# Copying operand stacks, row maxima and attention sums from SBUF to SBUF in a two-layer attention and FFN kernel

## The reference, cut to what matters

```python
x = x + attn_a(layernorm(x))      # (16, 512, 128) float32; 16 heads of 8; causal; three heads re-weighted by token region
x = x + ffn(layernorm(x))         # silu gate, two 512x512 layers with exact gelu, back to 128
x = x + attn_b(layernorm(x))      # 16 heads of 8; rotary; not causal
x = x + ffn(layernorm(x))
# one attention:
scores = einsum('bhqd,bhkd->bhqk', q, k) / sqrt(8)
out = einsum('bhqk,bhkd->bhqd', softmax(scores), v)       # then the output projection
```

## Time and profile before

| | us |
|---|---|
| median of 3 runs (2568.77 to 2573.33) | 2572.24 |
| the profiled execution | 2562.1 |
| its span | 2560.1 |
| attention "a", first maxima to last projection | 60.33 to 850.69 |
| attention "b", the same | 1308.22 to 2149.32 |

### The profile page before, as it was taken

How to read it: one execution, slowest core, us unless ns; L and a number is a source line. 1 busy time by engine, 2 the same in 40 slices (tenths; PEclk the granted TensorE clock), 3 DMA queues, 4 the chain that set the end, 5 groups by cost and what they waited for, 6 DMA issues and landing times. The chain is left out here.

```text
span 2560.1 us, 39181 instructions
## 1 busy us (share of the span) xinstructions
PE 2178.2 (85%) x14018; PEld 1036.9 (41%) x14018; DVE 1750.2 (68%) x2621; ACT 1463.2 (57%) x2948; POOL 984.6 (38%) x1184
## 2 busy tenths in 40 slices
PE   1889888888888599999658998998899874999998
PEld 0323223223222388788511222222222211888886
DVE  5766666666662467666259998998998852667663
ACT  0366556555556255555306777777777773555654
POOL 2445445445443244544332242232233200544543
PEclk8788878888887799999758999999999997999999
DMA  6343433433430000000033334434334310000000
GB/s 169 82 89 76 102 83 80 103 81 85 100 75 20 15 1 1 1 1 1 25 69 81 75 79 93 83 77 99 81 73 99 83 30 15 9 13 12 10 13 13
DMA packets 114582, 147.17 MB, mean 57 GB/s; under 512 B 27600, under 2 KB 88656, under 8 KB 113232
## 3 DMA queue, kind: packets, MB, share of 16 engines
q1 hardware_dynamic: 114384, 144.60, 26.0%
HBM read 78.47 MB, written 66.06 MB: 56 GB/s over the span
## 5 line engine op out<-in xcount | busy, mean ns | idle before, releaser
L586 DVE TENSOR_REDUCE b_negmax<-ps_max 128x2 f32<-128x1024 f32 x512 | 611.9, 1219 | 93.4 <-PE ps_max L700 90.9
L667 ACT ACTIVATE b_prob<-ps_score 128x512 f32<-128x512 f32 x1024 | 547.8, 598 | 196.0 <-PE ps_score L687 194.6
L586 DVE TENSOR_REDUCE a_negmax<-ps_max 128x2 f32<-128x256 f32 (+3 forms) x512 | 410.7, 821 | 225.6 <-PE ps_max L704 221.6
L667 ACT ACTIVATE a_prob<-ps_score 128x512 f32<-128x512 f32 (+3 forms) x1024 | 386.5, 437 | 302.0 <-PE ps_score L687 300.2
L687 PE MATMUL ps_score<-b_stack_q,stack_k 50*128 50x512 bf16 x1024 | 257.8, 388 | 56.1 <-ACT b_prob L667 46.8
L503 POOL TENSOR_SCALAR_AFFINE_SELECT a_prob<-a_prob 128x512 f32<-128x512 f32 x256 | 163.3, 638 | 363.4 <-ACT a_prob L667 363.4
L721 PE MATMUL ps_out<-b_prob,b_v_aug 128*9 128x512 f32 x2048 | 268.6, 596 | 18.9 <-ACT b_o_raw L640 12.9
L700 PE MATMUL ps_max<-stack_k,b_stack_q 48*128 48x512 bf16 x1024 | 233.9, 397 | 35.8 <-DMA stack_k<-d_stack 19.8
L687 PE MATMUL ps_score<-a_stack_q,stack_k 50*128 50x512 bf16 (+3 forms) x1024 | 204.1, 342 | 69.0 <-DMA a_stack_q<-d_nm 63.2
L980 PE MATMUL ps_score<-fa_h,w_hi 128*128 128x512 f32 x1024 | 251.6, 403 | 3.9 <-DVE fa_h L895 2.8
L980 PE MATMUL ps_score<-fb_h,w_hi 128*128 128x512 f32 x1024 | 247.5, 398 | 3.9 <-DVE fb_h L895 2.8
(11 more groups left out here) (136 smaller groups left out, 2946.9 us busy)
## 6 DMA issues: line engine op xcount, KB each, us to landing
stack_k<-d_stack SPq DMA_DIRECT2D x128, 192.0 KB, 4.2
d_stack<-a_parts SPq DMA_DIRECT2D x64, 192.0 KB, 2.8
a_stack_q<-d_stack SPq DMA_DIRECT2D x64, 192.0 KB, 4.5
d_stack<-b_parts SPq DMA_DIRECT2D x64, 192.0 KB, 2.8
b_stack_q<-d_stack SPq DMA_DIRECT2D x64, 192.0 KB, 4.1
d_stack<-a_parts SPq DMA_DIRECT2D x64, 128.0 KB, 2.8
d_stack<-b_parts SPq DMA_DIRECT2D x64, 128.0 KB, 2.8
d_stack<-a_parts SPq DMA_DIRECT2D x64, 64.0 KB, 2.5
```

The lines of the kernel that those rows point to most:

```text
L586: dve.tensor_reduce(m["negmax"][:, t, :, p], dve_banks("max", k)[:, :, 0:keys], AX.X, ALU.max, negate=True).then_inc(s["max"], 1)
L667: act.activation(m["prob"][u % PROBS][:, g, lo:S], act_bank("score", 4 * u + g)[:, 0:S - lo], ACT.Exp).then_inc(s["prob"], 1)
```

## The change

`d_stack`, `d_nm`, `d_num` and `d_den` in DRAM go away. The parts are copied straight into the stacks with 12 DMAs for q and 12 for k (`stack`), each from 64 partitions of `parts` (1 KB on each) to 8 partitions of a stack (8 KB on each). The rows of maxima, the sums and the numerators are copied straight as well; `o_num` in four DMAs, each from 8 partitions of `o_raw` (8 KB on each) to 32 partitions. The reciprocals still go through `d_rden`, read back in four DMAs instead of eight. There are three buffers of each stack instead of two, so that the copies of batch n wait for scores of batch n-3. SP's order becomes `aug(1)`, `numerators`, stack of q, reciprocals out, stack of k, reciprocals back, `aug(0)`. The first maxima of a batch wait for both whole stacks, no longer for a half. ScalarE waits for `den` and `o_in` before it overwrites `o_raw`. The rows of the output weights are reordered to match `o_num`, and the program reserves less scratch for DMAs.

```diff
@@ -44,6 +44,8 @@
 MASKED = -1.0e30
 SCORE_BANKS = 3
 PROBS = 4
+STACKS = 3
+COPIES = 16 * 2 * TERMS
 
 
 W_AT = {"a": 0, "b": F, "h1": 2 * F, "h2": 2 * F + FT * F, "out": 2 * F + 2 * FT * F}
...
-        m["d_stack"] = dram("d_stack", (2, 2, TERMS, HD, PAIRS, S), BF16)
-        m["d_nm"] = dram("d_nm", (2, 2, 2, HALF, S), BF16)
-        m["d_num"] = dram("d_num", (HD, 4, GROUPS, S), F32)
-        m["d_den"] = dram("d_den", (4, GROUPS, S), F32)
         m["d_rden"] = dram("d_rden", (4, GROUPS, S), F32)
...
@@ -347,69 +345,47 @@
             else:
                 sp.dma_start(m["focus"][:], a["focus"]).then_inc(s["focus"], 16)
 
-            def aug(h, b, c):
+            def aug(h, b):
 
                 sp.wait_ge(s[f"nm_row{h}"], b + 1)
-                sp.dma_start(m["d_nm"][h].rearrange("o c p t -> (o c p) t"), m["nm_rows"][:, h, :])\
-                    .then_inc(s["nm_out"], 16)
-
-                sp.wait_ge(s["nm_out"], count(32, b, 16 * (h + 1)))
                 for o in range(2):
                     at = SIDE * o + KROWS
-                    sp.dma_start(m["stack_q"][c][at:at + AUG, HALF * h:HALF * (h + 1), :],
-                                 m["d_nm"][h, o]).then_inc(s[f"aug{h}"], 16)
-
-            def outputs(b):
+                    sp.dma_start(m["stack_q"][b % STACKS][at:at + AUG, HALF * h:HALF * (h + 1), :],
+                                 m["nm_rows"][2 * HALF * o:2 * HALF * (o + 1), h, :]).then_inc(s[f"aug{h}"], 16)
+
+            def numerators(b):
 
                 sp.wait_ge(s["o_raw"], count(GROUPS, b, GROUPS))
+                wait(sp, s["rden"], b)
+                sp.dma_start(m["den"][:], m["o_raw"][HD::32]).then_inc(s["den"], 16)
+                wait(sp, s["oT"], b)
                 for g in range(4):
-                    sp.dma_start(m["d_num"][:, g], m["o_raw"][32 * g:32 * g + HD]).then_inc(s["o_out"], 16)
-                    sp.dma_start(m["d_den"][g:g + 1], m["o_raw"][32 * g + HD:32 * g + HD + 1])\
-                        .then_inc(s["o_out"], 16)
-                sp.wait_ge(s["o_out"], count(128, b, 128))
-                wait(sp, s["rden"], b)
-                sp.dma_start(m["den"][:], m["d_den"].rearrange("g h (c t) -> (g h c) t", c=P // H))\
-                    .then_inc(s["den"], 16)
-                wait(sp, s["oT"], b)
-                sp.dma_start(m["o_num"][:], m["d_num"].rearrange("d g h t -> (d g h) t")).then_inc(s["o_in"], 16)
+                    sp.dma_start(m["o_num"][32 * g:32 * (g + 1)], m["o_raw"][32 * g:32 * g + HD])\
+                        .then_inc(s["o_in"], 16)
+
+            def store_reciprocals(b):
+
                 sp.wait_ge(s["rden"], b + 1)
                 sp.dma_start(m["d_rden"].rearrange("g h (c t) -> (g h c) t", c=P // H), m["rden"][:])\
                     .then_inc(s["rden_out"], 16)
+
+            def spread_reciprocals(b):
+
                 sp.wait_ge(s["rden_out"], count(16, b, 16))
-                for d in range(HD):
-                    sp.dma_start(m["o_rden"][H * d:H * (d + 1), :], m["d_rden"].rearrange("g h t -> (g h) t"))\
-                        .then_inc(s["r_in"], 16)
-
-            def store(b):
-
-                for i, name in enumerate(("stored_q", "stored_k")):
-                    sp.wait_ge(s["parts"], count(2, b, i + 1))
-
-                    wait(sp, s["half0"], count(64, b))
-                    wait(sp, s["half1"], count(64, b))
+                for g in range(4):
+                    rows = m["d_rden"][g:g + 1].broadcast_to([HD, GROUPS, S])
+                    sp.dma_start(m["o_rden"][32 * g:32 * (g + 1)], rows).then_inc(s["r_in"], 16)
+
+            def stack(b, name, i):
+
+                wait(sp, s["score"], count(4 * UNITS, b - STACKS, 4 * UNITS))
+                sp.wait_ge(s["parts"], count(2, b, i + 1))
+                part_of = (0, 0, 0, 1, 1, 2) if i == 0 else (0, 1, 2, 0, 1, 0)
+                for t, part in enumerate(part_of):
                     for o in range(2):
-                        parts = m["parts"][64 * o:64 * (o + 1), i]
-                        rows = m["d_stack"][i, o].rearrange("t d p n -> (d p) t n")
-                        if i == 0:
-                            for part, lo, hi in ((0, 0, 3), (1, 3, 5), (2, 5, 6)):
-                                sp.dma_start(rows[:, lo:hi],
-                                             parts[:, part:part + 1].broadcast_to([64, hi - lo, S]))\
-                                    .then_inc(s[name], 16)
-                        else:
-                            for lo, hi in ((0, 3), (3, 5), (5, 6)):
-                                sp.dma_start(rows[:, lo:hi], parts[:, 0:hi - lo]).then_inc(s[name], 16)
-                sp.wait_ge(s["stored_q"], count(96, b, 96))
-                sp.wait_ge(s["stored_k"], count(96, b, 96))
-
-            def load(b, c, h):
-
-                wait(sp, s["score"], count(4 * UNITS, b - 2, 2 * UNITS * (h + 1)))
-                pairs = slice(HALF * h, HALF * (h + 1))
-                for o in range(2):
-                    q, k = (m["d_stack"][i, o].rearrange("t d p n -> (t d) p n") for i in range(2))
-                    rows = slice(SIDE * o, SIDE * o + KROWS)
-                    sp.dma_start(m["stack_q"][c][rows, pairs, :], q[:, pairs, :]).then_inc(s[f"half{h}"], 16)
-                    sp.dma_start(m["stack_k"][c][rows, pairs, :], k[:, pairs, :]).then_inc(s[f"half{h}"], 16)
+                        at = SIDE * o + HD * t
+                        sp.dma_start(m[name][b % STACKS][at:at + HD],
+                                     m["parts"][SIDE * o:SIDE * (o + 1), i, part]).then_inc(s[name], 16)
 
             if causal:
 
@@ -417,18 +393,20 @@
                     sp.dma_start(raw(i), a["w_" + name].rearrange("(k p) f -> p k f", p=P))\
                         .then_inc(s["w_raw"], 16)
             for n in range(STEPS):
-                c = n % 2
                 if on(n, 2):
-                    aug(1, n - 2, c)
+                    aug(1, n - 2)
                 if on(n, 3):
-                    outputs(n - 3)
+                    numerators(n - 3)
                 if on(n, 0):
-                    store(n)
-                    load(n, c, 0)
+                    stack(n, "stack_q", 0)
+                if on(n, 3):
+                    store_reciprocals(n - 3)
+                if on(n, 0):
+                    stack(n, "stack_k", 1)
+                if on(n, 3):
+                    spread_reciprocals(n - 3)
                 if on(n, 1):
-                    aug(0, n - 1, 1 - c)
-                if on(n, 0):
-                    load(n, c, 1)
+                    aug(0, n - 1)
 
         @block.gpsimd
         def _(pool):
...
-                wait(pool, s["stored_q" if i == 0 else "stored_k"], count(96, b))
+                wait(pool, s["stack_q" if i == 0 else "stack_k"], count(COPIES, b))
...
-                pool.wait_ge(s["o_in"], count(16, b, 16))
-                pool.wait_ge(s["r_in"], count(16 * HD, b, 16 * HD))
+                pool.wait_ge(s["o_in"], count(64, b, 64))
+                pool.wait_ge(s["r_in"], count(64, b, 64))
...
-                wait(act, s["nm_out"], count(32, b - 1, 16 * (h + 1)))
+                wait(act, s[f"aug{h}"], count(32, b))
...
-                wait(act, s["o_out"], count(128, b))
+                wait(act, s["den"], count(16, b))
+                wait(act, s["o_in"], count(64, b))
...
-                b, c = n - 2, n % 2
+                b, c = n - 2, (n - 2) % STACKS
...
-                    pe.wait_ge(s[f"half{h}"], count(64, b, 64))
...
             def maxes(n, k):
 
-                b, c = n - 1, (n - 1) % 2
+                b, c = n - 1, (n - 1) % STACKS
                 p, t = k // T, k % T
-                if k % (MAXES // 2) == 0:
-                    pe.wait_ge(s[f"half{k // (MAXES // 2)}"], count(64, b, 64))
+                if k == 0:
+                    pe.wait_ge(s["stack_q"], count(COPIES, b, COPIES))
+                    pe.wait_ge(s["stack_k"], count(COPIES, b, COPIES))
                 dve_banks_free(pe, n, "max", k)
                 to, keys = dve_banks("max", k), P * (t + 1) if causal else S
                 for o in range(2):
...
-    return np.array([(4 * G + g) * HD + d for d in range(HD) for g in range(4) for G in range(GROUPS)])
+    return np.array([(4 * G + g) * HD + d for g in range(4) for d in range(HD) for G in range(GROUPS)])
...
-    nc = bacc.Bacc("TRN2", target_bir_lowering=False, num_devices=1)
+    nc = bacc.Bacc("TRN2", target_bir_lowering=False, num_devices=1, dynamic_dma_scratch_size=1024)
```

More of the change, by code:

```diff
@@ L101, in program @@
         m["ps_max"] = ctx.enter_context(nc.psum_tensor("ps_max", [P, 4, 512], F32))
[L103 removed]
+        m["stack_k"] = [sb(f"stack_k{c}", [P, PAIRS, S], BF16) for c in range(STACKS)]
         m["ps_hid"], m["ps_misc"] = m["ps_score"][:, 0:2], m["ps_score"][:, 2]
@@ L158, in _ @@
             dve.memset(m["ps_out"][:], 0.0)
-            for c in range(2):
+            for c in range(STACKS):
```

(2 more changed lines are left out.)

7 lines of the change are left out of this document (3 added, 4 removed).

## The result

The changed kernel takes 2754.47 us (median of 4 runs, 2745.7 to 2758.44), the kernel before 2571.89 (4 runs): a ratio of 1.0707, 95% interval 1.0679 to 1.0735, 182.6 us slower. The profiled execution has a span of 2752.3 us against 2560.1.

The account below looks back on a forecast made before the run. It took the first attention to be bound by the wait for maxima and its half clock, no DMA bounding the second; 108 + 122 + 35 - 10 = +255 us on 2562.1 gave 2817, median 2827 us, range 2570 to 2995.

Parts of the forecast that it names:

- The price of a copy: Each 64 KB copy from 64 partitions to 8 takes 1.02 us, bounds 0.32 to 1.23; 24 take 24.5 us per step.
- the narrow stretch: Stretch from 835.7 to 840.2 in the earlier trace, four 64 KB copies from 8 partitions, 64 GB/s at DMA share 0.45.
- overlap between the halves: Consecutive copies, below and above partition 64 in turn, run beside each other: 0.55 us a copy, 2472 us; both fast cases 0.20.
- The reciprocals: Four DMAs spreading reciprocals, behind the copies in SP's queue: 3.0 us, four issues and 1.8 to land, before POOL's product.
- First attention: Copies, reciprocals, product, mask and two units form a loop: 55.4 us per step against 47.07, +108 us over 13 steps.
- the half clock that it put on the next step's start: First attention: of 3.7 us lost to half clock after unit 14's wait, 2.2 fall on the next step's start.
- Second attention: TensorE's projection in unit 14 waits for the product: 58.3 us per step against 48.88, +122 us over 13 steps.
- First batches: First maxima of the attentions +6.6 and +8.7 us later, the next two steps of each +5 each; together +35 us.
- Last batches: End of both attentions: without the DRAM hop, outputs to product take 10.9 us instead of 15.7; -10 us together.
- At nothing: Parts counted as costing nothing: third stack buffer, SP's 38 DMAs, ScalarE's new wait, larger clearing, first maxima's wait for whole stacks.
- The cheap rivals: Copies are cheap and the kernel faster: 0.32 us a copy gives 2446 us, 0.55 gives 2472; chance 0.20 for both.
- The break-even: Below 0.65 us per copy, about 100 GB/s, faster wins; there the two attention loops together equal 47.07 and 48.88 us.

Follow-up runs that it names:

- the best version: Changed kernel with rows six partitions apart and SP's order four q copies, reciprocals out, eight q copies, reciprocals spread, maxima, k's copies: 2499.47 us, ratio 0.9699.
- a better order: Changed kernel, rows still side by side, with reciprocals sent out within q's copies and reciprocals and maxima ahead of k's copies: 2574.38 us, ratio 0.9991.

## Why the prediction was right, and where it was off

It forecast 2827 us in a range of 2570 to 2995, slower at 0.77. Measured is 2754, in the direction and by the mechanism that it named, 28% less than the +255 us of its sum.

- **The price of a copy**, taken as 1.02 us from the narrow stretch of the earlier trace rows, is 0.92 by the windows of a slow step, about 0.7 in the fastest (91 to 104 GB/s), so the forecast had the slow end of it. Whether overlap between the halves, which it chose to ignore, makes the difference is not shown. With the reciprocals it said 27.5 us from q's part to the product; the trace has 26.0 at 341.61 and, in the second attention, 27.8 (1542.85 + 1.16 + 27.8 = 1571.81), but 24.7 and 26.1 in the mean of each attention's 13 steps.
- **The reciprocals**, taken as 3.0 us, were too cheap: with the copies bound by SP's issue, in the kernel with rows six apart, their way takes some 5.5. Copies too dear and reciprocals too cheap cancel in part in the 27.5; that part of the agreement is luck.
- **First attention**, 55.4 us per step forecast, 51.03 measured: +51 us instead of +108. This is the step that failed most. The failed term is the time from q's parts to the product, 24.7 us in the mean and not 27.5: 2.8 us of the gap of 4.4, and 1.5 in the step of the rows shown. Another 2.2 us are the half clock that it put on the next step's start: q's copies start at 368.05, 17.9 us after 350.17, which is the full-clock value, so the half clock was over by then. The two units after the wait took 6.6 us (343.60 to 350.17), not 5.9. With the mean, 17.9 + 24.7 + 1.9 + 6.6 is 51.1. The wait in unit 14, forecast as 13 us, is 7.3 to 13.0.
- **Second attention**, 58.3 us per step forecast, 58.37 measured. The loop is the plain sum that it named: in the step from 1519.78 it is 24.2 to q's part, 27.8, 1.3 for the product, 5.9 to the next step (forecast 5.3), 59.2 us, and some steps are shorter. That the mean meets the forecast to 0.1 us is luck.
- **First batches**: the two fills came as forecast (67.50 against 66.9; a wait 8.7 us longer at 1368.66, forecast +8.7). The +5 for each of the next two steps of an attention were not there: the first attention is 7.2 us late at its first maxima and 8.1 at 143.70, and the two steps after 1368.66 are 1.7 us longer together. So 18 us, not 35.
- **Last batches**, -10 forecast. From the marks at 747.58 and 807.07 to the last projection (850.69 and 903.35) the first attention's end is 6.8 us shorter, where -5 was forecast. The second's is 12 us longer by the clock, which no rival had; its wait for the product is 2.4 shorter.
- **At nothing.** "SP issues 38 DMAs per step instead of 45; the queue is bound by the engines behind it" was right for this kernel, 0.92 against 0.65 us, but hid the next limit: the stores in the earlier trace rows show it, 3.83 us for six, 0.64 each. The prediction even set a test by 24 times 0.3 us, the price of loads. With faster copies the issues bound at once. The third stack buffer can't be taken away alone: with two, SP would wait for the scores of batch n-2, which end with the step, ahead of the reciprocals on which that same step's masks depend. It wasn't tried.
- **The cheap rivals** (2446 and 2472 us) had the wrong condition but the right size of prize: the best version is at 2499. The break-even that they gave, 0.65 us per copy, holds only for the order in which the change put the queue, and not quite there: at the 0.65 us of the rows six apart the kernel was still 1.8% slower than before, with steps of 47.7 and 52.3 us where the sum's own terms give 46.5 and 49.4. In the second attention the 2.5 us that the reciprocals' term lacked are most of the difference; in the first they are partly made up, since q's parts are ready 17.9 us into the step and not 20.1. In a better order it broke even with the rows side by side.

## What to carry to other kernels

Saving a hop through DRAM is no gain by itself: look at how many partitions the narrow side of the direct copy has and how they are spread, since eight neighbours took 0.92 us per 64 KB in slow steps and eight rows two or six apart no more than the 0.65 of an issue. Then add up the issues of the queue, here 0.65 to 0.69 us for a reshaping copy of 64 KB as of 8 KB, from the first thing that becomes ready to the last that is waited for. Put what another engine waits for within the same step ahead of what is wanted only in the next, and send what needs a round trip out early enough that nobody stands still for its return.

## What the runs showed of the hardware

- An SBUF to SBUF copy between differently shaped sides cost SP 0.65 us of queue time for 64 KB and 0.69 for 8 KB (1.38 for two); 64 KB of numerators, in another shape, 0.83; the load of 192 KB from DRAM that the kernel before issues at 314.91 cost 0.42. Among these the cost goes with the form, not with the bytes.
- Copies of 64 KB to 8 neighbouring partitions, alternating between the halves of SBUF, ran at 66 to 87 GB/s in slow steps and 91 to 104 in fast ones, with a DMA share of 0.5 to 0.6. With the rows two or six partitions apart they ran at 88 to 105 GB/s, as fast as SP issued them, with a share of 0.32 to 0.37.
- The clock does not follow the length of the last wait alone: it fell to half after waits of 1.3 us (262.13) and not after another of 1.3 (392.55) in the same kernel, and in the changed kernel's last batch of the second attention it fell with no wait over 0.69 us since the one at the batch's start and stayed down for some 45 us. The same batch ran at 1.00 in the kernel before and in two versions of the changed one.
